# Pairs of PSUM banks as one tile in a block of causal attention and a gated feed-forward: one exp and one maximum per pair, the causal mask added by TensorE, and another place for the second half's maxima in the DMA queue

## The chip, the cores and the metric

The kernel runs on one core of one Trainium2 chip. The metric is device microseconds of that core, the median of several runs. Times inside the kernel come from one profiled execution, in microseconds (us) from the start of its span, or in ns where that is written.

## What is computed

Eight sequences (B) of 1024 tokens with 256 channels pass through a transformer block: a layer norm scaled and shifted per sequence, causal attention with 16 heads of 16 channels, a gated residual, a second modulated layer norm, and a feed-forward part that mixes each token with the one before it. The part that matters here:

```
scores = einsum("bhqd,bhkd->bhqk", q, k) * Hd ** -0.5
scores = where(causal, -inf, scores)
attn = softmax(scores)
out = einsum("bhqk,bhkd->bhqd", attn, v)
```

## The kernel before

**Tiling.** For each sequence `b` the heads are taken in four groups `s` of four. A group is worked off in twelve steps `t` (`COL_STEPS`). All engines walk the same list of (b, s, t), each with its own program in order, and semaphores tie them together. In the same steps stand the dense products of other parts of the block (projections for the next sequence, and output and feed-forward of the sequence before), so that a step holds attention work of three kinds and, mostly, a dense product.

**Column scores.** For a group's softmax weights TensorE makes scores with keys on partitions and queries along the free axis (`score_columns`, L1222 to L1240): `k_stack` is the stationary operand and `q_stack` the moving one, 64 rows each, so that an even head (rows 0 to 63) and an odd head (rows 64 to 127) use the two halves of the array at the same time. They go to two PSUM banks, `col_ps0` and `col_ps1`. A unit is one bank: one head where more than 256 queries are wanted, otherwise two. Eight of the twelve steps have four units, in two pairs; four steps have two units, one pair. ScalarE takes the exp of each unit (`exps`, L805 to L817), into `weights`. On diagonal blocks GpSimd sets the masked weights to zero (L664). TensorE multiplies the weights with `v_ones` (`values`, L1286), for step t in step t+1.

**Row maxima.** The softmax needs a maximum per query and head before the exp. It rides as two more rows of `q_stack`, and is worked out one group ahead: TensorE makes the scores of group s+1 with queries on partitions (`row_pair`, L1248 to L1269), into four banks `row_ps0` to `row_ps3`, and VectorE reduces them (`maximum`, L1021 to L1045). There are 40 units of one bank in a group, always an even and an odd one in a row. A unit whose block holds the diagonal goes through one masked add and maximum per head (L1035, a custom operation with `row_mask`, followed by a read of the accumulator); the others through a plain reduction (L1039). A group has 16 pairs of an even and an odd head whose block is diagonal. `split_max` (L1047 to L1067) then splits the maxima in two parts and turns them with one transpose of 128x32 in 32x32 blocks.

**The DMA queue.** SyncE issues nearly all transfers from one queue, in program order, and `hold` makes the whole queue wait. `fill_stacks` (L480 to L495) copies the next group's q and k into the stacks, twelve transfers per half of the tokens. `place_max` (L497 to L506) puts the turned maxima into `q_stack`, eight transfers per half: one for each 32 queries, for even and odd heads. Column scores of steps 0 and 4 wait for the two halves' maxima (L1226).

**TensorE's order in a step** (L1439 to L1465): the first pair of row scores (early), the first pair of column scores, the values of the step before, the second pair of row scores (late) if a dense product follows, the second pair of column scores, otherwise the late pair now, then the dense product.

## Time and profile before

| | |
|---|---|
| median of 3 runs | 1524.66 us (1518.13 to 1531.08) |
| profiled execution, its time | 1521.95 us |
| its span | 1520.0 us |
| busy PE, DVE, ACT, POOL | 1346.2, 1118.0, 958.2, 678.7 us |
| mean granted TensorE clock | 0.927 |

PE is TensorE, PEld its weight loads, DVE VectorE, ACT ScalarE, POOL GpSimd, SPq SyncE's DMA queue. Ends of matmuls are modelled and lie over each other, so that the time from one start to the next tells more than a duration. A granted clock of 1 is 2.4 GHz, of 0.5 it is 1.2 GHz.

### The profile page before, as it was taken

How to read it: one execution, taken by the hardware profiler on the slowest of the kernel's cores; microseconds unless marked ns; L12 is line 12 of the kernel's file. 1: busy time of each engine (PE TensorE's matmuls, PEld its weight loads, DVE VectorE, ACT ScalarE, POOL GpSimd, SP SyncE). 2: the span in 40 equal slices, each digit the busy share in tenths (PEclk: the TensorE clock that was granted, in tenths of full speed). 3: DMA queues.
4: the chain of work that ended last, by engine and by line, in shares of the span. 5: the costliest groups of instructions: out<-in, count | busy, mean ns of one | idle time of the engine just before them, and what ended most of it. 6: DMA issues, size and time to landing. Idle time of an engine off the chain costs nothing.

```text
span 1520.0 us, 28003 instructions
## 1 busy us (share of the span) xinstructions
PE 1346.2 (89%) x8744; PEld 746.3 (49%) x8744; DVE 1118.0 (74%) x3435; ACT 958.2 (63%) x1916; POOL 678.7 (45%) x1098
## 2 busy tenths in 40 slices
PE   5898889899998999889998899989998999998855
PEld 4443434455554555444554455545454555544444
DVE  8778667877678777877678777787778777777234
ACT  2167556766677666676677566776667666666633
POOL 4014122554436354553446545364546534343554
PEclk9598979999899999999899999999999898999878
DMA  4321124122331224222242223312232222221100
GB/s 139 75 64 47 42 50 112 49 65 68 84 86 46 54 66 118 67 54 55 67 108 53 56 70 97 82 44 54 72 105 63 64 54 76 68 58 50 38 29 28
DMA packets 90005, 101.77 MB, mean 67 GB/s; under 512 B 29681, under 2 KB 55545, under 8 KB 89857
## 3 DMA queue, kind: packets, MB, share of 16 engines
q1 hardware_dynamic: 89280, 99.20, 25.0%
q8 instruction: 70, 1.15, 0.3%
q10 hardware_dynamic: 576, 0.79, 0.3%
q14 instruction: 79, 0.64, 0.1%
HBM read 30.69 MB, written 8.94 MB: 26 GB/s over the span
## 4 chain that ended last, share of the span: by engine, by line
PE 51%; DVE 13%; SPq 10%; ACT 9%; issue 8%; POOL 7%; DMA 2%; ACTq 0%; POOLq 0%; DVEq 0%
PE val_ps L1286 13%; PE col_ps L1235 12%; PE row_ps L1264 9%; SPq L493 6%; ACT weights L815 5%; DVE row_ps L1035 5%; PE dense_ps L1296 4%; SPq L505 3%; PE dense_ps L1298 3%; PE dense_ps L1297 3%; PE dense_ps L1324 2%; DVE max_parts L1039 2%; POOL weights L664 2%; PE dense_ps L1339 2%; ACT xn_c L859 1%
## 5 line engine op out<-in xcount | busy, mean ns | idle before, releaser
L815 ACT ACTIVATE weights<-col_ps 128x512 f32<-128x512 f32 (+2 forms) x1280 | 643.7, 557 | 319.9 <-PE col_ps L1235 305.2
L1035 DVE CUSTOM_DVE_ANT_0 row_ps<-row_ps,row_mask 128x128 f32<-128x128 f32 (+3 forms) x1024 | 477.4, 517 | 209.7 <-PE row_ps L1264 209.3
L1235 PE MATMUL col_ps<-q_stack,k_stack 64*128 64x512 f32 (+3 forms) x1536 | 400.9, 410 | 36.1 <-ACT weights L815 20.4
L664 POOL TENSOR_SCALAR_AFFINE_SELECT weights<-weights 128x256 f32<-128x256 f32 x512 | 211.0, 425 | 460.1 <-ACT weights L815 458.7
L1039 DVE TENSOR_REDUCE max_parts<-row_ps 128x1 f32<-128x512 f32 x512 | 328.7, 681 | 86.5 <-PE row_ps L1264 84.8
L1286 PE MATMUL val_ps<-weights,v_ones 128*32 128x512 f32 (+3 forms) x3072 | 349.9, 529 | 25.6 <-POOL weights L664 18.1
L1264 PE MATMUL row_ps<-k_stack,q_stack 62*128 62x512 f32 (+3 forms) x1536 | 341.6, 434 | 29.3 <-DVE max_parts L1039 11.8
L1235 PEld LDWEIGHTS col_ps<-q_stack,k_stack 64*128 64x128 f32 x1536 | 210.5, 196 | 224.7 <-ACT weights L815 174.4
L1264 PEld LDWEIGHTS row_ps<-k_stack,q_stack 62*128 62x128 f32 x1536 | 163.8, 197 | 242.2 <-DVE max_parts L1035 79.9
L1035 DVE DVE_READ_ACCUMULATOR2_ANT max_parts<- 128x1 f32 x1024 | 144.7, 141 | 0.0
L1286 PEld LDWEIGHTS val_ps<-weights,v_ones 128*32 128x32 f32 x3072 | 62.1, 110 | 117.8 <-issue 61.6
L722 POOL TENSOR_TENSOR h_diff<-h 128x512 f32<-128x512 f32 x32 | 33.3, 1041 | 126.6 <-ACT h L878 125.9
L729 POOL TENSOR_TENSOR mix_lo<-mixed,mix_hi 128x512 fp32r<-128x512 f32 x64 | 81.7, 1298 | 17.5 <-ACT mix_hi L907 14.9
L1139 DVE SCALAR_TENSOR_TENSOR mixed<-h_diff,mus,h 128x256 f32<-128x256 f32 x128 | 63.8, 539 | 15.5 <-POOL h_diff L722 15.5
L1296 PE MATMUL dense_ps<-h_hi,w_hi 128*128 128x512 f32 x124 | 57.3, 462 | 3.0 <-POOL h_lo L639 1.6
L1298 PE MATMUL dense_ps<-h_hi,w_lo 128*128 128x512 f32 x124 | 51.7, 417 | 0.0
L733 POOL TENSOR_TENSOR k_lo<-k_sq,k_hi 128x512 fp32r<-128x512 f32 x28 | 39.3, 1404 | 26.4 <-ACT k_hi L912 25.9
L1297 PE MATMUL dense_ps<-h_lo,w_hi 128*128 128x512 f32 x124 | 51.0, 411 | 0.0
L888 ACT ACTIVATE h_diff<-dense_ps 128x512 f32<-128x512 f32 x28 | 16.7, 597 | 48.1 <-PE dense_ps L1345 48.1
L650 POOL TENSOR_SCALAR shift_c<-mv_c 128x2 f32<-128x2 f32 x32 | 8.5, 264 | 84.5 <-DVE mv_c L1076 84.1
L708 POOL TENSOR_TENSOR xq<-xq,gates_att 128x512 f32<-128x512 f32 x28 | 36.0, 1284 | 19.4 <-DMA xq<-in_x 19.3
L885 ACT ACTIVATE mix_out<-dense_ps 128x512 f32<-128x512 f32 x28 | 16.7, 598 | 38.4 <-PE dense_ps L1330 38.4
(194 smaller groups left out, 1893.8 us busy)
## 6 DMA issues: line engine op xcount, KB each, us to landing
q_stack<-q_part SPq DMA_DIRECT2D x384, 64.0 KB, 2.2
k_stack<-k_part SPq DMA_DIRECT2D x372, 64.0 KB, 2.2
xa<-in_x SPq DMA_DIRECT2D x8, 1024.0 KB, 5.6
q_stack<-max_rows SPq DMA_DIRECT2D x512, 2.0 KB
att<-val_out SPq DMA_DIRECT2D x64, 128.0 KB
recips<-recip_rows SPq DMA_DIRECT2D x32, 256.0 KB
xq<-in_x SPq DMA_DIRECT2D x28, 256.0 KB, 3.3
out<-xq SPq DMA_DIRECT2D x28, 256.0 KB, 2.1
```

The costliest lines, as they stand in the source:

```text
L493: sp.dma_start(stack[buf][at:at + HD, half].bitcast(F32), parts[part][lo:lo + 32, cols].bitcast(F32)).then_inc(stack_filled[buf][half], 16)
L664: nc.gpsimd.affine_select(out=w, in_=w, compare_op=ALU.is_ge, fill=0.0, base=0, pattern=[[0, 2], [1, P]], channel_multiplier=-1).then_inc( ...
L729: nc.gpsimd.tensor_tensor(mix_lo[:, m], mixed[:, m], mix_hi[:, m].bitcast(F32), ALU.subtract).then_inc(mix_lo_done, 1)
L815: nc.scalar.activation(weights[:, t % 2, heads[0]:heads[-1] + 1:2, 0:q1 - q0], col_ps[bank][:, 0:n * (q1 - q0)].rearrange("p (h q) -> p h ...
L1035: last = nc.vector.tensor_tensor_reduce(out=scores, in0=scores, in1=row_mask[:, HALF - width:HALF], scale=1.0, scalar=MASKED, op0=ALU.add, ...
L1039: last = nc.vector.reduce_max(dest, bank[:, 0:len(heads) * width].rearrange("p (h k) -> p h k", h=len(heads)), AX_X)
L1235: last = nc.tensor.matmul(col_ps[bank][:, i * (q1 - q0):(i + 1) * (q1 - q0)], stack_at(k_stack[s % 2], rows, heads[i], P * j, P * (j + 1)) ...
L1264: last = nc.tensor.matmul(banks[odd][:, n * width:(n + 1) * width], stack_at(q_stack[stack], rows, heads[n], P * i, P * (i + 1)), stack_at ...
L1286: last = nc.tensor.matmul(val_ps[32 * h:32 * h + 32, q0 - base:q1 - base], v_ones[:, j, G * s + h].rearrange("p d a -> p (d a)"), weights[ ...
L1296: nc.tensor.matmul(dst, a_hi(c), b_hi(c), start=(c == 0), stop=False)
L1297: nc.tensor.matmul(dst, a_hi(c), b_lo(c), start=False, stop=False)
L1298: last = nc.tensor.matmul(dst, a_lo(c), b_hi(c), start=False, stop=(c == KC - 1))
```

## The change

- The two column banks become one tile `col_ps` of two banks, and the four row banks two tiles of two banks. `exps` takes both units of a pair in one ACTIVATE of up to 1024 elements and waits for both; `maximum` reduces both units of a pair in one TENSOR_REDUCE and waits for both. The counts of semaphores stay, in steps of two.
- The custom masked maximum is gone. On diagonal blocks TensorE adds the mask to the scores in PSUM, with products of two bf16 constants (an identity and a triangle of -3e38), for even and odd heads side by side: per pair of heads four more matmuls, two with 128 columns and two with 64.
- The maxima are turned with four transposes of 32x32 into one tile of 32 partitions, so that `place_max` needs two transfers instead of eight.
- SyncE issues `place_max` of the second half right behind `fill_stacks`, ahead of the residual's load and the copies of values and sums.

The core of the diff:

```diff
-PLACED = 2 * (P // SQUARE) * 16
+PLACED = 2 * 16
 ...
+        col_pair = ps("col_ps", [P, COL_BANKS, HALF])
+        row_pair_ps = [ps(f"row_ps{i}", [P, 2, HALF]) for i in range(ROW_BANKS // 2)]
 ...
-                    for q in range(P // SQUARE):
-                        lo = SQUARE * q + 8 * MROWS * odd
-                        sp.dma_start(rows[:, :, q, :], max_rows[half][lo:lo + 8 * MROWS, :]
-                                     ).then_inc(max_placed[half], 16)
+                    sp.dma_start(stack[row:row + MROWS, half].rearrange("p g n -> p (g n)").bitcast(F32),
+                                 max_rows[half][8 * MROWS * odd:8 * MROWS * (odd + 1), :]).then_inc(max_placed[half], 16)
 ...
-                act.wait_ge(cols_ready, exp_index(b, s, c) + 1)
+                act.wait_ge(cols_ready, exp_index(b, s, c) + 2)
 ...
-                nc.scalar.activation(weights[:, t % 2, heads[0]:heads[-1] + 1:2, 0:q1 - q0],
-                                     col_ps[bank][:, 0:n * (q1 - q0)].rearrange("p (h q) -> p h q", h=n),
-                                     ACT.Exp, scale=SCALE).then_inc(exp_done, 1)
+                nc.scalar.activation(weights[:, t % 2, heads[0]:heads[0] + 2 * n, 0:q1 - q0].rearrange(
+                    "p (n o) q -> p o n q", o=2), col_pair[:, :, 0:n * (q1 - q0)].rearrange(
+                    "p o (n q) -> p o n q", n=n), ACT.Exp, scale=SCALE).then_inc(exp_done, 2)
 ...
-                        last = nc.vector.tensor_tensor_reduce(
-                            out=scores, in0=scores, in1=row_mask[:, HALF - width:HALF], scale=1.0, scalar=MASKED,
-                            op0=ALU.add, op1=ALU.max, accum_out=dest[:, n:n + 1])
+                nc.vector.reduce_max(dest, banks[:, :, 0:n * (k1 - k0)].rearrange("p o (n k) -> p o n k", n=n), AX_X
+                                     ).then_inc(max_done, 2)
 ...
-                nc.vector.transpose(max_rows[half][:], parts[:, 0:SQUARE].bitcast(F32)).then_inc(max_turned, 1)
+                for q in range(P // SQUARE):
+                    cols = slice(SQUARE * q, SQUARE * (q + 1))
+                    last = nc.vector.transpose(max_rows[half][:, cols], parts[cols, 0:SQUARE].bitcast(F32))
+                last.then_inc(max_turned, 1)
 ...
+                for n in range(len(pair[0])) if diagonal else ():
+                    for a in range(2):
+                        for odd in range(2):
+                            rows = slice(ROW_TILE * odd, ROW_TILE * (odd + 1))
+                            end = n == len(pair[0]) - 1 and a == 1
+                            last = nc.tensor.matmul(banks[odd][:, (n + 1) * width - P + ROW_TILE * a:(n + 1) * width],
+                                                    mask_ident[rows, a, :], mask_fill[rows, a, ROW_TILE * a:P],
+                                                    start=False, stop=end, skip_group_check=True)
+                            if end:
+                                last.then_inc(rows_ready, 1)
```

SyncE's part (`hold(max_turned, ...)` and `place_max(q_stack[s % 2], 1)` move up in `body`) is shown by its queue. Here is a group of the first sequence that also has back work; `xq` is the residual, `att` and `sums` the copies of values and sums. Before:

```order
L493 DMA k_stack0<-k_part0 16x2x512 x2
L493 DMA k_stack0<-k_part1 16x2x512 x2
L493 DMA k_stack0<-k_part0 16x2x512 x2
L534 DMA xq1<-in_x 128x2x256
L512 DMA att<-val_out1 64x512 [waits att_done,val_copied]
L514 DMA sums1<-val_out1 32x1x64
L505 DMA q_stack1<-max_rows1 2x8x32 [waits max_turned]
L505 DMA q_stack1<-max_rows1 2x8x32 x7
L539 DMA out<-xq0 128x2x256 [waits out_done]
```

The same place of the change:

```order
L496 DMA k_stack0<-k_part0 16x2x512 x2
L496 DMA k_stack0<-k_part1 16x2x512 x2
L496 DMA k_stack0<-k_part0 16x2x512 x2
L504 DMA q_stack1<-max_rows1 2x8x128 [waits max_turned]
L504 DMA q_stack1<-max_rows1 2x8x128
L533 DMA xq1<-in_x 128x2x256
L511 DMA att<-val_out1 64x512 [waits att_done,val_copied]
L513 DMA sums1<-val_out1 32x1x64
L538 DMA out<-xq0 128x2x256 [waits out_done]
```

The maxima move from behind three transfers and two waits to directly behind the fills, and are two rows instead of eight.

TensorE at steps 0 and 1 of a group (`row_ps` row scores, `col_ps` column scores, `val_ps` values). Before:

```order
L1235 MATMUL col_ps<-q_stack,k_stack 128x512 [waits exp_done,max_placed0]
L1235 MATMUL col_ps<-q_stack,k_stack 128x512 [waits exp_done]
L1286 MATMUL val_ps<-weights,v_ones 32x128 [waits sel_done]
L1286 MATMUL val_ps<-weights,v_ones 32x128 x3
L1235 MATMUL col_ps<-q_stack,k_stack 128x512 [waits exp_done] x2
L1264 MATMUL row_ps<-k_stack,q_stack 128x256 [waits max_done] x2
L1264 MATMUL row_ps<-k_stack,q_stack 128x256 x2
L1264 MATMUL row_ps<-k_stack,q_stack 128x384 [waits max_done] x2
L1235 MATMUL col_ps<-q_stack,k_stack 128x384 [waits exp_done] x2
```

The same place of the change:

```order
L1232 MATMUL col_ps<-q_stack,k_stack 128x512 [waits exp_done] x2
L1262 MATMUL row_ps<-k_stack,q_stack 128x256 [waits max_done] x2
L1262 MATMUL row_ps<-k_stack,q_stack 128x256 x2
L1273 MATMUL row_ps<-mask_fill,mask_ident 128x128 x2
L1273 MATMUL row_ps<-mask_fill,mask_ident 128x64 x2
L1273 MATMUL row_ps<-mask_fill,mask_ident 128x128 x2
L1273 MATMUL row_ps<-mask_fill,mask_ident 128x64 x2
L1262 MATMUL row_ps<-k_stack,q_stack 128x384 [waits max_done] x2
L1273 MATMUL row_ps<-mask_fill,mask_ident 128x128 x2
L1273 MATMUL row_ps<-mask_fill,mask_ident 128x64 x2
L1232 MATMUL col_ps<-q_stack,k_stack 128x384 [waits exp_done] x2
```

The order of scores and values is the same; behind each diagonal row pair there are four mask matmuls per pair of heads, ahead of the next column scores.

## Rows read from the trace of the kernel before

**Rows 1.** The page: busy us of each engine, share of the span, instructions
```profile
PE 1346.2 (89%) x8744; PEld 746.3 (49%) x8744; DVE 1118.0 (74%) x3435; ACT 958.2 (63%) x1916; POOL 678.7 (45%) x1098
```
**Rows 2.** The page's chain that ended last, by engine and by line
```profile
PE 51%; DVE 13%; SPq 10%; ACT 9%; issue 8%; POOL 7%; DMA 2%; ACTq 0%; POOLq 0%; DVEq 0%
PE val_ps L1286 13%; PE col_ps L1235 12%; PE row_ps L1264 9%; SPq L493 6%; ACT weights L815 5%; DVE row_ps L1035 5%; PE dense_ps L1296 4%; SPq L505 3%; PE dense_ps L1298 3%; PE dense_ps L1297 3%; PE dense_ps L1324 2%; DVE max_parts L1039 2%; POOL weights L664 2%; PE dense_ps L1339 2%; ACT xn_c L859 1%
```
**Rows 3.** Stretches: length, busy PE, PEld, DVE, ACT, POOL, then granted clock
```profile
40.00:70.00 30.00, 25.58 (x60) 13.77 (x60) 25.72 (x92) 2.31 (x5) 0.34 (x1) 0.50 0.35 63
500.00:700.00 200.00, 184.81 (x1239) 101.44 (x1238) 154.74 (x483) 135.41 (x273) 97.16 (x157) 0.96 0.26 68
```
**Rows 4.** Groups: line, engine, shapes, count, busy us, mean ns, idle before
```profile
L815 ACT ACTIVATE weights<-col_ps 128x512 f32<-128x512 f32 x896 | 488.1, 601 | 192.6 <-PE col_ps L1235 180.7
L1035 DVE CUSTOM_DVE_ANT_0 row_ps<-row_ps,row_mask 128x128 f32<-128x128 f32 (+3 forms) x1024 | 477.4, 517 | 209.7 <-PE row_ps L1264 209.3
L1035 DVE CUSTOM_DVE_ANT_0 row_ps<-row_ps,row_mask 128x512 f32<-128x512 f32 x256 | 172.1, 713 | 69.8 <-PE row_ps L1264 69.7
L1035 DVE CUSTOM_DVE_ANT_0 row_ps<-row_ps,row_mask 128x128 f32<-128x128 f32 x256 | 66.6, 320 | 24.8 <-PE row_ps L1264 24.8
L1039 DVE TENSOR_REDUCE max_parts<-row_ps 128x1 f32<-128x512 f32 x512 | 328.7, 681 | 86.5 <-PE row_ps L1264 84.8 <-issue 0.2
L1067 DVE STREAM_TRANSPOSE max_rows<-max_parts 128x32 f32<-128x32 f32 x64 | 13.5, 212 | 2.2
```
**Rows 5.** Timeline, a group's step 0: start, length, engine, line
```profile
670.85 0.30 PEld L1264 LDWEIGHTS row_ps<-k_stack,q_stack 62*128 62x128 f32 x4
...
671.07 0.19 PEld L1235 LDWEIGHTS col_ps<-q_stack,k_stack 64*128 64x128 f32 x2
...
671.61 2.27 ACT L815 ACTIVATE weights<-col_ps 128x512 f32<-128x512 f32 x4
...
672.26 0.18 PEld L1235 LDWEIGHTS col_ps<-q_stack,k_stack 64*128 64x128 f32 x1 [0.60 <-ACT weights L815]
...
672.75 0.18 PEld L1235 LDWEIGHTS col_ps<-q_stack,k_stack 64*128 64x128 f32 x1 [0.30 <-ACT weights L815]
```
**Rows 6.** Timeline, a step with a dense product of six matmuls
```profile
702.72 1.08 ACT L815 ACTIVATE weights<-col_ps 128x512 f32<-128x512 f32 x2
...
703.61 0.74 PE L1235 MATMUL col_ps<-q_stack,k_stack 64*128 64x512 f32 x2
...
704.15 1.09 ACT L815 ACTIVATE weights<-col_ps 128x512 f32<-128x512 f32 x2 [0.35 <-PE col_ps L1235]
704.28 0.19 PEld L1296 LDWEIGHTS dense_ps<-h_hi,w_hi 128*128 128x128 f32 x1 [0.24 <-issue]
```
**Rows 7.** Timeline, two matmuls of 512 columns behind each other
```profile
700.76 0.39 PE L1297 MATMUL dense_ps<-h_lo,w_hi 128*128 128x512 f32 x1
...
700.99 0.39 PE L1298 MATMUL dense_ps<-h_hi,w_lo 128*128 128x512 f32 x1
```
**Rows 8.** Timeline, SyncE's queue and TensorE up to step 4 of the group
```profile
676.95 0.50 SPq L534 DMA_DIRECT2D xq<-in_x  x1
...
678.91 5.27 SPq L505 DMA_DIRECT2D q_stack<-max_rows  x8
...
684.49 0.44 PE L1264 MATMUL row_ps<-k_stack,q_stack 62*128 62x128 f32 x3 [0.74 <-DVE max_parts L1039]
...
685.27 0.50 PE L1235 MATMUL col_ps<-q_stack,k_stack 64*128 64x512 f32 x2 [0.35 <-DMA q_stack<-max_rows]
```
**Rows 9.** Waits: who waited for whom, us in total, times, longest
```profile
PE col_ps L1235 <- DMA q_stack<-max_rows: 12.8, 10, 3.1
```
**Rows 10.** The chain in order of time, start of a group s = 1
```profile
627.89 0.32 DVE row_ps L1035
...
629.04 1.01 DVE att_n L1154
...
632.20 0.62 DVE stats_a L1072 x2
```

More of the change, by code:

```diff
@@ L160, in build @@
         max_parts = [sb(f"max_parts{i}", [P, P], F32R) for i in range(2)]
-        max_rows = [sb(f"max_rows{i}", [P, 2 * MROWS * 8]) for i in range(2)]
+        max_rows = [sb(f"max_rows{i}", [SQUARE, P]) for i in range(2)]
         val_out = [sb(f"val_out{i}", [P, HALF]) for i in range(2)]
@@ L919, in body @@
                     units = range(COL_FIRST[t], COL_FIRST[t + 1]) if attends(kind) else ()
-                    for c in units[:2]:
+                    for c in units[:1]:
                         exps(b, s, t, c)
@@ L924, in body @@
                     normalise_next(b, kind, s, t)
-                    for c in units[2:]:
+                    for c in units[2::2]:
                         exps(b, s, t, c)
@@ L1180, in body @@
                         empty_dense(*item)
-                    for u in early[1:]:
-                        maximum(b, s, u)
                     for item in at:
                         mix(*item)
-                    for u in late:
+                    for u in late[::2]:
                         maximum(b, s, u)
@@ L1262, in row_pair @@
                         rows = slice(ROW_TILE * odd, ROW_TILE * odd + MAX_AT)
-                        end = n == len(heads) - 1
+                        end = n == len(heads) - 1 and not diagonal
                         last = nc.tensor.matmul(banks[odd][:, n * width:(n + 1) * width],
@@ L1269, in row_pair @@
                             last.then_inc(rows_ready, 1)
+                for n in range(len(pair[0])) if diagonal else ():
+                    for a in range(2):
+                        for odd in range(2):
+                            rows = slice(ROW_TILE * odd, ROW_TILE * (odd + 1))
+                            end = n == len(pair[0]) - 1 and a == 1
[4 more added lines that the diff above has]
+                                last.then_inc(rows_ready, 1)
             def values(b, s, t):
```

61 lines of the change are left out of this document (29 added, 32 removed).

## The prediction

> **What bounds the kernel now.** The page's first part comes first: TensorE is busy 89% of the span, VectorE 74%, ScalarE 63% [rows 1]. The chain that ended last says that this is not TensorE alone: half of it (51%) is TensorE, 13% VectorE, 10% SyncE's queue, 9% ScalarE, 7% GpSimd [rows 2]. So I read stretches. In the middle (500 to 700 us) TensorE is busy 185 of 200 us at a granted clock of 0.96, close to the 2.4 GHz level; in the opening (40 to 70 us) VectorE and TensorE are both busy for 25.6 and 25.7 of 30 us, but at a clock of 0.50, the 1.2 GHz level, and there only row scores and maxima run [rows 3]. The reader is to see that in the middle work added to TensorE is paid unless it falls into one of its waits, and that work taken from VectorE or ScalarE pays only where TensorE waits for it.
>
> The timeline of a step shows two such patterns. In a step with a dense product [rows 6] the second pair of column scores starts at 703.61 and its second matmul stands waiting for the second exp (0.74 us for the pair against 0.50 for a pair that starts together [rows 8]); the dense product follows at 704.28 and hides the exps from 704.15 on. In a step without one [rows 5] the four exps run as one unbroken chain of 2.27 us, because TensorE gets the first bank back 0.49 us ahead of the second (672.26 and 672.75) and refills it while ScalarE works on the other.
>
> **The change part by part. The mask on TensorE.** 16 pairs of heads per group, 32 groups, are 512 pairs of heads, each with two pairs of matmuls (128 and 64 columns). No row shows a bf16 operand. From above: row pairs of 128 columns go at the pace of their loads, two pairs from 670.85 until the next load at 671.07, so 0.11 us a pair and 0.22 per pair of heads [rows 5]. From below: 512 columns take 0.23 us from start to start [rows 7], so 128 take 0.057 and 64 take 0.028, together 0.085, if the loads are hidden. The first mask load can hide behind the row product, but the load of whatever follows cannot hide behind 64 columns; and the operand has half the bytes. No row says whether a load goes by bytes or by columns, so I take the middle, 0.15.
>
> The Trainium skill bears on this (TensorE: Matmul & The Clock Gate, section on weight-path perf modes): it says that loads of 128 columns in a type other than fp32 are made about twice as fast. By that, the load of a mask would take an estimated 0.055 us and a pair of heads about 0.165 (0.055 and then the next fp32 load's 0.11); by the row it is 0.22. No row here shows which; by the first the term below would be 58 us, by the second 77.
>
> On the path lie those in steps where TensorE is not waiting anyway. In twelve steps they stand as 4, 2, 2, 0, 2, 0, 2, 1, 1, 0, 1, 1. The two late ones of step 0 run behind the second column scores while the exps are awaited, and I count three more as absorbed by waits (step 4, and in groups s = 1 and 3 where chains of other engines end last). That leaves 11 of 16: 32 x 11 x 0.15 = **53 us more**.
>
> **One exp per pair.** Two exps of 512 behind each other take 1.08 us [rows 6], one takes 0.60 [rows 4]; another 512 elements add 0.48 to that from the same two rows, or a little less without the second start, so one of 1024 is worth about 1.04, a gain of 0.04 a pair. The price is that TensorE gets both banks at once. From the start of a load to the first exp are 0.54 us (671.07 to 671.61 [rows 5]), and this gap can no longer lie beside an exp: two pairs take 1.04 + 0.55 + 1.04 = 2.63 us instead of 2.27, **0.36 us more**, wherever nothing else lies in between. With a dense product it costs nothing: the second pair's second matmul waited for the second exp already, TensorE reaches the dense product at the same 704.28, and the exps end 0.1 us later beside 1.4 us of dense work [rows 6, 7]. If that cover were gone it would cost the same 0.36. By the program, 10 of the 48 steps of a sequence have four units and no dense product. Eight sequences: 80 x 0.36 = **29 us more**. What is queued behind the waiting column scores on TensorE are the late rows and the next step; who waits for them are ScalarE and VectorE.
>
> **One maximum per pair.** The busy time of maxima is 477.4 + 328.7 = 806 us [rows 4]. The reads of the accumulator lie within. One column more costs (172.1 - 66.6) / 256 / 384 = 1.07 ns, a reduction of 512 costs 328.7 / 512 = 0.64 us, so one of 1024 costs 1.19 and one of 768 costs 0.92. A group has 14 pairs of 1024, 4 of 768 and 2 of 512: 21.6 us, 691 in all, 115 less. Three more transposes per half, at most 0.21 each [rows 4], give back up to 40. So VectorE is relieved of some 75 us, but it waits for row scores for 210 + 87 us already [rows 4], so this counts only where it ends last. One place is the opening, where it is as busy as TensorE [rows 3]: about 4 us. The other is the start of group s = 1, where from 627.89 to 632.20 eight masked maxima and one other operation of 1.01 are the chain [rows 10]: 3.3 us become 0.64 + 1.19, 1.4 less, in seven sequences 10 us. **14 us less.** A first pair of maxima now stands whole ahead of the dense unit's emptying on VectorE, where only half of it did: that emptying comes 0.5 us later. TensorE claims the dense bank again only behind two pairs of column scores and the values, and the masks delay it by as much; I take nothing.
>
> **The placement of maxima.** Eight transfers take 5.27 us of the queue, 0.66 each, and stand behind 1.96 us of residual, values and sums (676.95 to 678.91) [rows 8]. Two take 1.3, so the second half's maxima land 5.9 us earlier, and the last wait of column scores at step 4 goes: 12.8 us in ten waits [rows 9]. Next in line there is VectorE, which held the row scores ahead of it 0.74 us [rows 8], and that stays. Values and sums come 1.3 us later by the move, with a whole group until the next use of their buffer, so nothing. **13 us less.** The exps that are on the chain (5% of the span [rows 2], 76 us or some 66 pairs) give 3 us by their 0.04, and fewer long waits of TensorE may leave it at 2.4 GHz a little more often; 5 us for that is a guess from the 4% missing in the clock [rows 3]. Together **8 us less**. GpSimd gets a few small operations more, once, at its start, where the loads of weights and tokens are under way; I take nothing.
>
> **Sum.** 53 + 29 - 14 - 13 - 8 = +47 on the profiled execution's 1521.95 us (1520.0 span and 1.95 around it), which is 2.7 below the median of the runs: 1569, and with half of that difference **1570 us**.
>
> **Rivals.** *The reliefs win* (other side). If the mask products cost only their columns (0.085) and half of them fall into waits, they are 256 x 0.085 = 22 us; the coupling in half of its steps 15; and if half of the 115 us that the maxima lose lies on the path, 57, with 13 and 8 as above, the sum is -41: 1481 us. It decides where more than about 95 us of relief reach the path against the full 53 and 29. For it speaks that VectorE is 13% of the chain and SyncE's queue 10% [rows 2]; against it that VectorE waits for TensorE far more than the other way round [rows 4]. *Nothing that can be measured*: masks at 0.10 (35 us) and coupling 29 against 60 of relief, +4: 1526. *Lockstep everywhere*: if the dense products do not hide the coupling, it is paid in all eight four-unit steps of each group, 256 x 0.36 = 92, and the masks fully, 512 x 0.22 = 113; with 35 of relief +170: 1692. Against it speaks the second matmul that waits already [rows 6].
>
> **How the numbers follow.** I give the forecast 0.55, nothing measurable 0.20, the reliefs 0.15, lockstep 0.10. A measurement of this kernel tells about 1% from no change, which is 1509 to 1540. So faster 0.15, same 0.20, slower 0.65. The forecast's own range, with masks between 0.085 (30 us) and 0.22 on all (113), is 1540 to 1630. The range to be given reaches from 1510 to 1630: below it lies most of the reliefs' 0.15, above it most of lockstep's 0.10, about 0.2 together.
>
> **What would show it.** In the profile after: the mask line's matmuls with about 0.15 us per pair of heads from the end of the row product's columns to the next start; in a step 0 a gap near 0.55 us on ScalarE between its two exps; no wait of column scores for the placements of maxima; VectorE's busy share down to about 68%, with more waiting for row scores; the first row maxima earlier in the opening. The prediction is wrong if the mask loads are hidden (then TensorE's time hardly grows), if ScalarE's gaps show up behind dense products too, or if stretches where other engines end last shorten by more than 1.5 us per group.

## The result, and the profile after

The changed kernel takes 1573.8 us (median of 4 runs, 1570.8 to 1579.7) against 1522.8 us for the kernel before (1518.1 to 1531.1): a ratio of 1.0333 with a 95% interval of 1.0278 to 1.0389. A second comparison later gave 1.0279 (1.0244 to 1.0314). So the change costs 43 to 51 us; forecast were 47. The profiled execution has 1573.96 us, a span of 1572.1. Two executions on record ran in a slower state of the chip, one of the kernel before (1546.32 us) and one of the kernel without masks at the old place (1508.59 us), and the ratios leave them out.

Two lines of the page: busy us by engine, and the chain that ended last by engine:

```profile
PE 1311.9 (83%) x10792; PEld 740.3 (47%) x10792; DVE 1057.9 (67%) x1707; ACT 919.4 (58%) x1276; POOL 673.9 (43%) x1102
...
PE 50%; ACT 18%; DVE 14%; issue 10%; POOL 6%; DMA 1%; SPq 1%; ACTq 1%; POOLq 0%; DVEq 0%
```

Every engine is busy for less time than before [rows 1], TensorE too, although it has 2048 matmuls more, and yet the span is 52 us longer: what grew is waiting. (TensorE's sum is of modelled durations, at a mean granted clock of 0.938 for 0.927, so it does not say what the masks cost.) On the chain ScalarE went from 9 to 18% and SyncE's queue from 10 to 1% [rows 2]. The groups by line, busy us and mean ns, then the idle time before them with what ended it, say where:

```profile
L1036 DVE TENSOR_REDUCE max_parts<-row_ps 128x2 f32<-128x1024 f32 (+3 forms) x640 | 704.7, 1113 | 399.1 <-PE row_ps L1273 307.1 <-PE row_ps L1262 90.6 <-issue 0.2
L819 ACT ACTIVATE weights<-col_ps 128x1024 f32<-128x1024 f32 (+2 forms) x640 | 600.3, 938 | 425.9 <-PE col_ps L1232 383.4 <-issue 39.1
L1232 PE MATMUL col_ps<-q_stack,k_stack 64*128 64x512 f32 (+3 forms) x1536 | 306.3, 423 | 114.9 <-ACT weights L819 112.4
L1232 PEld LDWEIGHTS col_ps<-q_stack,k_stack 64*128 64x128 f32 x1536 | 143.4, 194 | 267.3 <-ACT weights L819 259.7 <-issue 1.0
L1273 PE MATMUL row_ps<-mask_fill,mask_ident 64*128 64x128 bf16 (+1 forms) x2048 | 115.4, 214 | 0.0
L1273 PEld LDWEIGHTS row_ps<-mask_fill,mask_ident 64*128 64x128 bf16 x2048 | 58.0, 99 | 40.8 <-issue 24.9
L1065 DVE STREAM_TRANSPOSE max_rows<-max_parts 32x32 f32<-32x32 f32 x256 | 51.2, 200 | 4.9
```

The exps (L819) and the column scores (L1232) wait for each other: ScalarE 383 us for scores, and the scores' matmuls 112 us for exps. Before, the matmuls waited 20 us for exps and 13 us for placements [rows 9]:

```profile
ACT weights L815 <- PE col_ps L1235: 305.2, 254, 25.2
...
PE col_ps L1235 <- ACT weights L815: 20.4, 59, 0.7
```

The wait for placements is gone. The maxima take 705 us instead of 806 [rows 4], close to what was worked out (691), and the four transposes 51 instead of 13.5.

### The profile page after: what moved, and what is told of

It is laid out like the page before. It is cut to its first block, busy times and chain, and to the rows that moved or that the text cites. A ratio compares the mean times of both kernels' runs of the same rounds, so it can differ in the third digit from the quotient of the medians.

```text
span 1572.1 us, 30252 instructions
## 1 busy us (share of the span) xinstructions
PE 1311.9 (83%) x10792; PEld 740.3 (47%) x10792; DVE 1057.9 (67%) x1707; ACT 919.4 (58%) x1276; POOL 673.9 (43%) x1102
## 4 chain that ended last, share of the span: by engine, by line
PE 50%; ACT 18%; DVE 14%; issue 10%; POOL 6%; DMA 1%; SPq 1%; ACTq 1%; POOLq 0%; DVEq 0%
ACT weights L819 13%; PE col_ps L1232 12%; PE val_ps L1294 9%; PE row_ps L1262 8%; DVE max_parts L1036 8%; PE dense_ps L1304 4%; PE dense_ps L1332 3%; PE dense_ps L1305 3%; PE dense_ps L1306 3%; POOL weights L669 2%; PE row_ps L1273 2%; PE dense_ps L1347 2%; PE dense_ps L1323 2%; ACT xn_c L863 2%; POOL mix_lo L734 1%
## 5 line engine op out<-in xcount | busy, mean ns | idle before, releaser
L1036 DVE TENSOR_REDUCE max_parts<-row_ps 128x2 f32<-128x1024 f32 (+3 forms) x640 | 704.7, 1113 | 399.1 <-PE row_ps L1273 307.1
L819 ACT ACTIVATE weights<-col_ps 128x1024 f32<-128x1024 f32 (+2 forms) x640 | 600.3, 938 | 425.9 <-PE col_ps L1232 383.4
L1232 PE MATMUL col_ps<-q_stack,k_stack 64*128 64x512 f32 (+3 forms) x1536 | 306.3, 423 | 114.9 <-ACT weights L819 112.4
L1262 PE MATMUL row_ps<-k_stack,q_stack 62*128 62x512 f32 (+3 forms) x1536 | 302.0, 426 | 26.0 <-DVE max_parts L1036 17.8
L1232 PEld LDWEIGHTS col_ps<-q_stack,k_stack 64*128 64x128 f32 x1536 | 143.4, 194 | 267.3 <-ACT weights L819 259.7
L1262 PEld LDWEIGHTS row_ps<-k_stack,q_stack 62*128 62x128 f32 x1536 | 143.5, 194 | 218.4 <-issue 127.5
L1273 PE MATMUL row_ps<-mask_fill,mask_ident 64*128 64x128 bf16 (+1 forms) x2048 | 115.4, 214 | 0.0
L1138 DVE SCALAR_TENSOR_TENSOR mixed<-h_diff,mus,h 128x256 f32<-128x256 f32 x128 | 65.0, 548 | 20.4 <-POOL h_diff L727 20.4
L1273 PEld LDWEIGHTS row_ps<-mask_fill,mask_ident 64*128 64x128 bf16 x2048 | 58.0, 99 | 40.8 <-issue 24.9
L1065 DVE STREAM_TRANSPOSE max_rows<-max_parts 32x32 f32<-32x32 f32 x256 | 51.2, 200 | 4.9
L713 POOL TENSOR_TENSOR xq<-xq,gates_att 128x512 f32<-128x512 f32 x28 | 35.9, 1284 | 25.8 <-DMA xq<-in_x 25.8
L1304 PE MATMUL dense_ps<-w_hi,h_hi 128*128 128x256 f32 x120 | 38.2, 318 | 5.8 <-DVE xq L1121 5.8
```

Of the source, the lines that this page charges most:

```text
L819: nc.scalar.activation(weights[:, t % 2, heads[0]:heads[0] + 2 * n, 0:q1 - q0].rearrange("p (n o) q -> p o n q", o=2), col_pair[:, :, 0:n ...
L1036: nc.vector.reduce_max(dest, banks[:, :, 0:n * (k1 - k0)].rearrange("p o (n k) -> p o n k", n=n), AX_X).then_inc(max_done, 2)
L1138: last = nc.vector.scalar_tensor_tensor(mixed[:, m, c, :], h2_diff[:, c, :], mus[:, m, c:c + 1], h2[s % 2][:, c, 0:QT], ALU.mult, ALU.add)
L1232: last = nc.tensor.matmul(col_ps[bank][:, i * (q1 - q0):(i + 1) * (q1 - q0)], stack_at(k_stack[s % 2], rows, heads[i], P * j, P * (j + 1)) ...
L1262: last = nc.tensor.matmul(banks[odd][:, n * width:(n + 1) * width], stack_at(q_stack[stack], rows, heads[n], P * i, P * (i + 1)), stack_at ...
L1273: last = nc.tensor.matmul(banks[odd][:, (n + 1) * width - P + ROW_TILE * a:(n + 1) * width], mask_ident[rows, a, :], mask_fill[rows, a, RO ...
```

## The experiments

All ratios are to the kernel before, run beside each kernel; 1% is 15.3 us of its median of some 1529 us. Differences between two kernels are differences of such ratios. A stretch in the tables below runs from the first product of one step's values to that of the next; "behind step 5" is the stretch that starts with the values of step 5. It holds the second pair of column scores and the dense product of step 6.

### An exp for each bank again

In the changed kernel (PE, SyncE and VectorE as they are):

```diff
-                act.wait_ge(cols_ready, exp_index(b, s, c) + 2)
+                act.wait_ge(cols_ready, exp_index(b, s, c) + 1)
...
-                nc.scalar.activation(weights[..., heads[0]:heads[0] + 2 * n, ...], col_pair[:, :, ...], ...).then_inc(exp_done, 2)
+                nc.scalar.activation(weights[..., heads[0]:heads[-1] + 1:2, ...], col_ps[bank][...], ...).then_inc(exp_done, 1)
...
-                    for c in units[:1]:
+                    for c in units[:2]:
```

> The changed kernel with one thing undone: each column bank has its own exp again (640 become 1280), the first bank is freed half an exp earlier. Masks on TensorE, paired maxima, two transfers per placement and their early place stay. Theory A, the terms of the prediction: the coupling costs 29 us less the 3 us of exps that were on the chain, so 26 come back: about 1548 us. Theory B, which the trace after suggests (ScalarE's waits for column scores grew from 305 to 383 us, TensorE's waits for exps to 112): the coupling is the larger term, 50 to 60 us, and the masks the smaller: about 1515 to 1522. Rival C, coupling free: stays at 1574. In A and B the wait of column scores for exps falls from 112 us to near the 20 of before.

Measured: 1517.05 us, ratio 0.9924 (0.9895 to 0.9954). The pairing of exps is worth the whole loss and more: 3.6 to 4.1%, some 54 to 63 us. That is theory B for the coupling. The waits, us in total, times, longest:

```profile
ACT weights L820 <- PE col_ps L1233: 305.7, 360, 25.7
...
PE col_ps L1233 <- ACT weights L820: 19.8, 61, 0.7
```

Both are back where they were before (305.2 and 20.4).

The price shows in a step without a dense product. Timeline of step 0 of a group in the changed kernel, start and length in us, the idle time before in brackets:

```profile
832.56 1.02 ACT L819 ACTIVATE weights<-col_ps 128x1024 f32<-128x1024 f32 x1 [0.35 <-PE col_ps L1232]
...
833.64 0.19 PEld L1232 LDWEIGHTS col_ps<-q_stack,k_stack 64*128 64x128 f32 x2 [1.11 <-ACT weights L819]
833.64 0.50 PE L1232 MATMUL col_ps<-q_stack,k_stack 64*128 64x512 f32 x2 [0.84 <-ACT weights L819]
...
834.22 0.35 PE L1273 MATMUL row_ps<-mask_fill,mask_ident 64*128 64x128 bf16 x8
834.26 1.02 ACT L819 ACTIVATE weights<-col_ps 128x1024 f32<-128x1024 f32 x1 [0.68 <-PE col_ps L1232]
```

The exp ends at 833.58, TensorE starts to load 0.06 later, and the second exp starts at 834.26: a gap of 0.68 us, of which 0.62 lie between the load and the exp. That is longer than the 0.54 of [rows 5]. This exp needs both banks, but the two matmuls start together, so the wait for the second explains little of the 0.08, and what does stays open. The two exps span 832.56 to 835.28, 2.72 us, where four took 2.27 [rows 5].

### The mask products left out

In the changed kernel:

```diff
-                diagonal = k1 == P * (i + 1)
+                diagonal = False
```

> The changed kernel without the mask products on TensorE: the row maxima are then taken over the whole diagonal tile, so this kernel leaves the mask out. Paired exps and all else stay. Theory A, the prediction's term: 0.15 us per pair of heads on 11 of 16, 53 us come back: about 1521. Theory B: the loads of the masks are nearly hidden, 0.085 per pair of heads, 30 us or less come back: 1544 or more. Rival C: each product and the next load cost their full loads, 0.22: about 1496.

Measured: 1562.1 us, ratio 1.0209 (1.0168 to 1.0250); the changed kernel in its two comparisons 1.0333 and 1.0279. The masks cost 11 to 19 us in the changed kernel, the smaller with intervals that overlap. That is on theory B's side, and below the 30 us that it had as its most. Two stretches of one sequence show where they cost and where not (length, busy PE, PEld, DVE, ACT, POOL, granted clock, DMA share, GB/s). The changed kernel, from the values of step 10 to those of step 11, and from those to the next group's:

```profile
829.31:832.38 3.07, 3.07 (x35) 2.28 (x35) 2.46 (x9) 1.20 (x2) 0.77 (x2) 1.00 0.28 64
832.38:835.92 3.54, 2.15 (x32) 1.30 (x31) 1.80 (x2) 2.68 (x4) 0.81 (x2) 1.00 0.45 103
```

The same two without masks:

```profile
815.39:818.23 2.84, 2.84 (x26) 2.05 (x27) 2.32 (x9) 0.98 (x2) 0.77 (x2) 1.00 0.30 69
818.23:821.78 3.55, 1.78 (x21) 0.97 (x19) 2.00 (x3) 2.74 (x5) 0.82 (x2) 1.00 0.43 100
```

In the first TensorE never waits, and two pairs of heads cost 0.23 us, 0.115 each. In the second three pairs of heads cost nothing (3.54 and 3.55): their columns lie in the gap that the paired exp opens. The granted clock over the whole span fell as well, from 0.938 to 0.909 in the profiled executions (in the others 0.926 to 0.942 with masks, 0.907 to 0.921 without). So some stretches are longer without the masks, at the lower clock. Behind step 3 of group 1, with masks and then without:

```profile
666.00:669.55 3.55, 1.90 (x18) 0.86 (x17) 3.41 (x8) 2.72 (x4) 3.24 (x6) 1.00 0.22 74
650.39:654.55 4.16, 2.79 (x18) 1.27 (x16) 3.58 (x9) 2.90 (x5) 3.60 (x6) 0.67 0.19 63
```

Part of what the masks cost is given back that way; how much was not measured.

### The old place in SyncE's queue

In the changed kernel, hold and place_max of the second half go back behind residual, values and sums:

```diff
-                    if attends(kind):
-                        hold(max_turned, b * (2 * G) + (2 * s + 2))
-                        place_max(q_stack[s % 2], 1)
                     if backs(kind) and kind != "drain":
                         load_residual(b, s)
...
+                    if attends(kind):
+                        hold(max_turned, b * (2 * G) + (2 * s + 2))
+                        place_max(q_stack[s % 2], 1)
                     if attends(kind) and s == G - 1:
                         load_gates(b)
```

> The changed kernel with SyncE's issue of the second half's maxima put back behind residual, values and sums. Two transfers per placement stay. Theory A: two transfers instead of eight end about 4.0 us earlier by themselves (0.66 us each), more than the mean stall of 1.28 us that the column scores had, so the place in the queue is worth nothing: 1574, within 3 us. Rival B: the place is what took the stall away: 12.8 us come back, about 1587, and a wait of column scores for the placements stands in the profile again in about ten steps.

Measured: 1567.18 us, ratio 1.0253 (1.0215 to 1.0291), not above the changed kernel (1574, to be met within 3, was 7 us off). No wait of column scores for placements shows up. Two transfers at the old place are early enough, so rival B falls; no gain of the new place shows, and it may cost some us.

### The changed kernel beside the others

> The changed kernel once more, beside the others, to compare it with the one that has the old place (1.0253). Theory A: the early place costs a little, since residual and values stand behind it: 1.033 again. Rival B: the difference was that of two jobs: 1.025 to 1.028.

Measured: 1570.83 us, ratio 1.0279 (1.0244 to 1.0314). That is in rival B's range. Against 1.0253 at the old place it is within the intervals: the place is worth between nothing and a loss of 0.8%; the sign stays open.

### The new place alone, in the kernel before

The same lines moved up in the kernel before, where place_max issues eight transfers.

> The kernel before with one thing of the change alone: SyncE issues the second half's eight transfers of maxima behind the stack fills, ahead of residual, values and sums. Theory A: they land about 1.96 us earlier, more than the mean stall of 1.28 us in ten steps, so 10 to 13 us are gained: about 1511. Rival B: residual, values and sums now come 5.3 us later, and what they feed (residual into the dense step, values into the next buffer) waits: no gain or a loss, 1523 or more. Rival C: the stall was hidden behind another wait, 1523.

Measured: 1650.08 us, ratio 1.0792 (1.0753 to 1.0830): 121 us slower. Rival B had the mechanism, but nobody had the size. The waits in it:

```profile
PEld val_ps L1286 <- POOL weights L664: 165.2, 127, 6.0
POOL xq L708 <- DMA xq<-in_x: 146.1, 28, 7.7
PE val_ps L1286 <- POOL weights L664: 131.7, 51, 5.9
```

and the same in the kernel before:

```profile
PEld val_ps L1286 <- POOL weights L664: 48.6, 110, 1.5
...
POOL xq L708 <- DMA xq<-in_x: 19.3, 17, 2.4
PE val_ps L1286 <- POOL weights L664: 18.1, 38, 1.4
```

The residual xq is issued behind eight transfers and so comes late. GpSimd waits for it in 28 steps, and behind that wait in GpSimd's queue stand the selects of the diagonal weights; TensorE's values wait for these, 114 us more. The granted clock of the span fell to 0.875. It is the transfers that make the residual late, some 5.3 us of the queue each time, and not the wait for the turned maxima that now stands ahead of it too: SyncE waited for those twice, once for 18.3 us.

```profile
SPq L131 <- DVE max_rows L1067: 27.5, 2, 18.3
```

With two transfers ahead of it the same order is nearly free: GpSimd's wait for the residual is 25.8 us in the changed kernel, and 1.8 with the old place.

### An exp for each bank at the old place

Both edits above together in the changed kernel.

> The changed kernel with two things undone: an exp per column bank, and the second half's maxima issued behind residual, values and sums again. What stays of the change: masks on TensorE, paired maxima, four transposes and two transfers per placement. Theory A, the effects add: 0.76% below the kernel before from the exps alone, and 6 us more from the old place: about 17 us below the kernel before, ratio 0.989. Rival B: the old place helped only because TensorE stood in the coupling; then the ratio stays at 0.992 or rises.

Measured: 1516.9 us, ratio 0.9922 (0.9895 to 0.9948), the same as with the new place. Theory A's 0.989 lies just outside the interval; with an exp per bank no worth of the place can be measured. Taking the pairing of exps from the kernel at the old place gives 1.0253 - 0.9922 = 3.3%, 51 us.

### The same without masks

> As the kernel with an exp per bank and the old place, but without the mask products: the maxima are taken over whole diagonal tiles, so the mask is left out. It prices the masks where the coupling doesn't hide them. Theory A: in the steps of the trace a pair of heads cost 0.09 to 0.135 us, so 352 on the path give back 32 to 48 us: ratio to the kernel before about 0.965. Rival B: as with paired exps, a TensorE with less to do is granted a lower clock (0.909 against 0.938 there) and gives most of it back: ratio within 0.012 of the kernel with the masks.

Measured: 1498.89 us, ratio 0.9793 (0.9738 to 0.9848). Here the masks cost 1.3%, 20 us, short of theory A and at the edge of what B allowed (1.2%). The granted clock is 0.952 against 0.966 with them in the profiled executions; over all executions in the ratios the medians are 0.951 and 0.960, and their ranges overlap. So the masks look dearer where exps don't open gaps for them, and cost some two fifths of the term forecast.

This is the quickest kernel of all those measured. One thing follows for the mask: GpSimd still sets the masked weights to zero behind the exp, and in exact arithmetic a softmax does not depend on which maximum is subtracted, so a maximum over the whole tile will do as long as masked scores aren't so much larger that the exps of the others vanish. For which inputs that holds no run here shows.

### Two transfers and four transposes alone, in the kernel before

```diff
-PLACED = 2 * (P // SQUARE) * 16
+PLACED = 2 * 16
...
-                nc.vector.transpose(max_rows[half][:], parts[:, 0:SQUARE].bitcast(F32)).then_inc(max_turned, 1)
+                for q in range(P // SQUARE):
+                    cols = slice(SQUARE * q, SQUARE * (q + 1))
+                    last = nc.vector.transpose(max_rows[half][:, cols], parts[cols, 0:SQUARE].bitcast(F32))
+                last.then_inc(max_turned, 1)
```

with place_max as in the changed kernel, at its old place.

> The kernel before with one thing of the change: four transposes per half instead of one, and two transfers per placement instead of eight, at their old place in SyncE's queue. Theory A: the stall of 12.8 us in ten waits goes, since the transfers end about 4 us earlier, and what stands behind the 5.3 us of eight transfers (loads of tokens, the next stack fills) comes earlier too: 10 to 15 us less, ratio 0.991. Rival B: the three more transposes (40 us of VectorE in all) stand in front of the next maxima and eat the gain: ratio 0.997 or more.

Measured: 1537.87 us, ratio 1.0067 (1.0040 to 1.0094): 10 us slower. The wait for placements is gone and nothing is gained. TensorE's matmuls of row scores wait longer for maxima instead:

```profile
PE row_ps L1263 <- DVE max_parts L1035: 24.3, 33, 1.3
...
PE row_ps L1263 <- DVE max_parts L1031: 9.1, 13, 2.3
```

In the kernel before:

```profile
PE row_ps L1264 <- DVE max_parts L1039: 11.8, 17, 0.9
...
PE row_ps L1264 <- DVE max_parts L1035: 5.8, 10, 1.0
```

That is 33.4 us for 17.6. The transposes stand in VectorE's order ahead of maxima whose banks TensorE needs. Behind step 2 of group 3 of one sequence (length, busy PE, PEld, DVE, ACT, POOL, granted clock, DMA share, GB/s), in the kernel before and then with the four transposes:

```profile
904.25:907.23 2.98, 2.11 (x18) 1.00 (x17) 2.95 (x7) 0.66 (x2) 2.26 (x4) 1.00 0.07 23
915.27:918.85 3.58, 2.04 (x18) 0.93 (x16) 3.47 (x10) 0.66 (x2) 2.85 (x4) 1.00 0.29 73
```

VectorE is busy nearly all the time in both, and the stretch is 0.60 us longer, as much as three more transposes of 0.2 us. Behind step 2 of groups 0, 2 and 3 it is longer in most sequences. The lower clock behind them comes and goes between executions, so the 10 us were not added up from them.

### One exp per pair alone, in the kernel before

> The kernel before with one thing of the change: one exp over both column banks. Prices the coupling alone. Theory A, as it came out of the changed kernel: about 0.55 us in each four-unit step without a dense product and some more around it, 50 to 57 us: ratio about 1.035. Theory B, the prediction's working: 0.36 us in 80 steps, less 3: ratio 1.017. Rival C: the coupling costs only beside the masks, ratio 1.005 or less.

Measured: 1565.55 us, ratio 1.0249 (1.0210 to 1.0287): 38 us, between theories A and B. TensorE's column scores wait 116.2 us for exps. Rival C falls: the masks are not needed for the coupling.

### One transpose and eight transfers, with paired maxima

The kernel with an exp per bank at the old place, with the transposes and transfers of the kernel before.

> The changed kernel with three things undone: an exp per bank, the old place in SyncE's queue, and one transpose with eight transfers per placement. What stays of the change: masks on TensorE and one maximum per pair of banks. Theory A, effects add: two transfers with four transposes cost 0.67% in the kernel before, so without them 0.9922 - 0.0067 = 0.9855 of the kernel before. Rival B: paired maxima have taken VectorE off that path, so the transposes cost nothing now, and the ratio stays at 0.992. Rival C: with eight transfers the wait of the column scores for placements comes back and costs 13 us: 1.000.

Measured: 1526.41 us, ratio 0.9992 (0.9966 to 1.0018), 0.7% above the kernel with two transfers: rival C. The wait is back:

```profile
PEld col_ps L1234 <- DMA q_stack<-max_rows: 10.2, 8, 3.2
PE col_ps L1234 <- DMA q_stack<-max_rows: 8.9, 8, 3.0
```

So the same edit costs 10 us in the kernel before and gains 11 with paired maxima and masks on TensorE. The reading is that VectorE was next in line there and no longer is here; which of the two took it out of line was not tested apart.

### One maximum per bank

The kernel with an exp per bank at the old place, with maxima of one bank each; masks on TensorE, transposes and transfers stay as in the change. With it the second maximum of a step's first pair stands behind the emptying of the dense bank again, as in the kernel before.

```diff
-                dve.wait_ge(rows_ready, at + 2)
+                dve.wait_ge(rows_ready, at + 1)
...
-                nc.vector.reduce_max(dest, banks[:, :, 0:n * (k1 - k0)]..., AX_X).then_inc(max_done, 2)
+                nc.vector.reduce_max(dest, bank[:, 0:len(heads) * (k1 - k0)]..., AX_X).then_inc(max_done, 1)
```

> The kernel with an exp per bank and the old place (ratio 0.992), with the pairing of maxima undone as well: one maximum per bank, 1280 instead of 640; masks on TensorE, four transposes and two transfers stay. It prices the pairing. Theory A, what the sum of the other runs leaves: masks 20, transposes 10, and 42 us of gain by the paired maxima, so 1.02 of the kernel before. Theory B, the prediction: 14 us, ratio 1.001. In A the stretches behind step 2 of groups 2 and 3, where the granted clock fell in the kernel before, are long again.

Measured: 1545.41 us, ratio 1.0100 (1.0068 to 1.0132). The pairing of maxima gains 1.8%, 27 us: between the theories, and twice what the prediction gave to all of the maxima. Stretches around step 2 of group 2 show it (columns as above). Maxima of one bank each:

```profile
868.89:872.51 3.62, 2.27 (x27) 1.15 (x25) 3.55 (x9) 0.67 (x3) 2.89 (x4) 1.00 0.00 0
872.51:877.39 4.88, 4.88 (x23) 2.91 (x22) 3.25 (x10) 3.20 (x6) 1.29 (x4) 0.65 0.22 78
```

Paired maxima:

```profile
855.41:857.61 2.20, 1.94 (x26) 0.97 (x25) 2.17 (x4) 0.66 (x2) 1.55 (x3) 1.00 0.00 0
857.61:861.54 3.93, 3.37 (x25) 1.95 (x23) 3.69 (x8) 3.22 (x6) 1.75 (x2) 1.00 0.20 66
```

And the kernel before:

```profile
859.06:862.85 3.79, 2.28 (x16) 1.03 (x16) 3.79 (x13) 0.26 (x1) 3.26 (x4) 0.88 0.02 3
862.85:868.82 5.97, 5.97 (x24) 3.30 (x23) 2.72 (x9) 3.26 (x6) 1.47 (x5) 0.51 0.21 70
```

In the kernel before VectorE is busy all 3.79 us of the first stretch and TensorE only 2.28. Then the granted clock falls to 0.51, the 1.2 GHz level, and the next stretch takes 5.97 us instead of 3.93. That this is the clock shows in the kernel before itself, where the second sequence has the same stretch at 1.00:

```profile
334.06:337.99 3.93, 3.93 (x24) 2.05 (x23) 3.47 (x16) 3.22 (x6) 1.45 (x2) 1.00 0.20 67
```

The long step is paid twice: by the wait, and by the clock behind it. It is not so in every sequence: behind step 3 of group 2 the kernel before has 5.16 to 5.97 us at 0.51 to 0.70 in six of eight, and with paired maxima two of eight are that long. The Trainium skill (TensorE: Matmul & The Clock Gate, section on HAM oscillation) tells of the same for waits on transfers: work behind a long wait starts at the lower clock. The trace agrees, 0.51 behind a wait that is on another engine, VectorE.

### One exp per pair only beside a dense product

The kernel with an exp per bank at the old place, paired where a four-unit step has a dense product:

```diff
+                dense_at = {(unit[0], unit[1]) for unit in dense_units(b, kind)}
...
+                    both = len(units) == 4 and (s, t) in dense_at
+                    for c in units[:2:2 if both else 1]:
+                        exps(b, s, t, c, both)
```

> The kernel with an exp per bank and the old place (ratio 0.992), but with one exp per pair of banks in the four-unit steps that have a dense product behind the second column scores, and only there. Theory A, the prediction's step: beside a dense product the pairing costs nothing, and it saves ScalarE a start: 0.992, or up to 3 us less. Rival B: part of the 51 us of pairing was paid in those steps too: 1.00 or more. In A the four-unit steps with a dense product last as long as with an exp per bank (3.61 and 3.87 us behind steps 5 and 7 of group 0), and those without one 3.0 instead of 3.55.

Measured: 1523.65 us, ratio 0.9964 (0.9942 to 0.9986) against 0.9922 without any pairing: between the theories, nearer to A. Stretches behind steps 5 and 7 of group 0 and step 5 of group 3, with this pairing, and (the third) behind step 11 of group 0, which has no dense product and an exp for each bank here:

```profile
783.69:787.27 3.58, 3.01 (x23) 1.32 (x21) 2.92 (x4) 3.39 (x6) 0.00 (x0) 1.00 0.50 165
791.48:795.37 3.89, 3.69 (x22) 1.69 (x20) 2.46 (x4) 2.54 (x3) 0.82 (x2) 1.00 0.41 95
804.76:807.77 3.01, 2.54 (x32) 1.60 (x31) 1.31 (x2) 2.80 (x6) 0.81 (x2) 1.00 0.46 106
...
913.12:916.67 3.55, 2.99 (x21) 1.32 (x20) 1.77 (x3) 3.39 (x6) 3.34 (x5) 1.00 0.01 2
```

The same with an exp for each bank:

```profile
776.67:780.29 3.62, 3.05 (x23) 1.48 (x21) 2.98 (x4) 3.52 (x8) 0.00 (x0) 1.00 0.58 169
784.55:788.42 3.87, 3.87 (x23) 1.87 (x21) 2.45 (x4) 2.67 (x5) 0.83 (x2) 1.00 0.44 102
797.80:800.80 3.00, 2.53 (x32) 1.59 (x31) 1.30 (x2) 2.80 (x6) 0.82 (x2) 1.00 0.46 107
...
906.99:910.31 3.32, 3.22 (x21) 1.35 (x20) 2.03 (x3) 3.25 (x8) 3.17 (x5) 1.00 0.01 2
```

Steps 5 and 7 last the same with one exp or two (3.58 and 3.62, 3.89 and 3.87), and the step without a dense product is at 3.0 again. In a few others, as behind step 5 of group 3, the pairing costs 0.2 to 0.3 us although work on the dense bank is there. The difference in all is 0.4%, 6 us, with intervals that just overlap; it was not followed further. So most of the 51 us that the pairing of exps costs come from the other steps: the four-unit steps without such work, and the steps of two units, which have an exp for each bank in this kernel as well.

## Why the prediction was right

The time, 1574 for a forecast 1570, is right; the sum under it is right only as a whole, since errors of its terms cancel. That they cancel to within a few us is luck. What was rightly seen is that the change loses, that the coupling of the exps and the masks cost more than the reliefs give, and where the coupling is paid. One way of adding up the change, from the kernel before to the changed one, each step from two measured ratios:

| step | ratio after it | us | the prediction's terms |
|---|---|---|---|
| four transposes, two transfers | 1.0067 | +10 | -13, with the place |
| masks from VectorE to TensorE, one maximum per bank | 1.0100 | +5 | +53, less a part of 14 |
| one maximum per pair | 0.9922 | -27 | part of -14 |
| one exp per pair | 1.0253 | +51 | +29, less 3 |
| the new place | 1.0279 | +4, not clear of noise | in the -13 |

The second row is a difference of two edits at once (1.0100 - 1.0067) and within both intervals; the others stand on one edit each. Another order gives other numbers, because the effects don't add: transfers and transposes cost 10 us in one kernel and gain 11 in another, and the pairing of exps costs 38 and 51, there with intervals that overlap.

**The masks, 53 forecast.** The direction was right; of the size some two fifths or less are left. A pair of heads costs 0.115 us where TensorE is the bound, not 0.15, and nothing in the steps where an exp is awaited. Taken out, they give back 20 us with an exp per bank and 11 to 19 in the changed kernel. The rule of the Trainium skill cited ahead of the result (TensorE: Matmul & The Clock Gate, weight-path perf modes) agrees on the load, 99 ns recorded for a bf16 load against 194 for fp32; but the estimate from it, 0.165 a pair, is too high. The 0.115 lies nearer to the 0.085 that the prediction gave to the columns alone, so most of the loads seems to lie beside columns.

**The coupling, 29 forecast.** It is the largest term, not the second. The mechanism was as described: a gap between two exps in steps without a dense product, next to nothing in most steps with one. Three things were mis-sized. First, the gap is 0.68 us, not 0.55: 0.62 from the load to the exp where the working took 0.54, and TensorE's start behind the first exp, 0.06, which it left out. Second, the end of the chain moves the next step's first column scores as well, since they need both banks: such a step lasts 3.54 us for 3.00, 0.54 more and not 0.36. That holds for step 0 of a group, and for most of the same kind at step 4. At steps 8 and 9 most are 0.03 to 0.31 longer. Behind step 8 of group 0, which holds step 9, with an exp for each bank and then in the changed kernel (columns as above):

```profile
788.42:791.39 2.97, 2.90 (x24) 1.28 (x22) 2.94 (x5) 2.47 (x7) 0.82 (x2) 1.00 0.46 105
822.90:825.96 3.06, 2.56 (x25) 1.04 (x23) 3.03 (x5) 2.35 (x5) 0.81 (x2) 1.00 0.46 107
```

Third, there are more such steps than 80. The 10 are right for the middle sequences, but by the program the first has 18, the second 11 and the last 19, since part of the dense work of their neighbours is missing there: 98 in all. Added up stretch by stretch, from the profiled execution with an exp for each bank (new place) to that of the changed kernel's second comparison, the 98 are 40 us longer, 0.41 each, of the 50 by which the spans differ; in the kernel before, with and without the pairing, 38 of 45. So the term should have been about 40. The rest lies in the other steps, mainly four-unit steps beside dense products, which the prediction had free; what makes it was not found.

**The maxima, 14 less forecast.** The busy time was right (705 us for 691), and the place of the gain was not: it was sought in the opening and at the start of group s = 1. The opening gained nothing: in the trace TensorE's first values start at 75.5 us of the span, before at 73.8, and the first maximum at 45.0 for 44.0. Without the masks the first values start at 72.3, so there, at a granted clock of 0.50, the masks take more than the maxima give. The gain lies mainly around step 2 of groups 2 and 3, where VectorE was full and TensorE fell to the lower clock behind it. "It waits for row scores already, so this counts only where it ends last" was the right rule; the prediction looked for such places in two stretches alone, and named the price of the clock as a guess of 5 us.

**The placement, 13 less forecast.** This step failed. The wait was indeed gone, as forecast, but VectorE stood next in line, which the prediction said too, and yet it counted the full 12.8 us as gain. In the kernel before the edit costs 10 us, as TensorE waits longer for maxima behind three more transposes; the prediction had put them off the path as a part of 75 us of relief. Only with paired maxima and masks on TensorE do two transfers gain about what was forecast, 11 us. The earlier place in the queue, which was to bring 1.96 of the 5.9 us by which the maxima land earlier, gives nothing that shows.

**The last 8 less.** Neither part was found. The 3 us by longer exps don't show: with exps paired beside dense products alone the time is 6 us longer, barely clear of noise, and not shorter. The 5 us by the clock were a guess; the granted clock is 0.938 for 0.927, and no run tells what that alone is worth.

**SyncE's queue.** "Values and sums come 1.3 us later, so nothing" was right as far as the waits show, in which nothing for these two grew by more than 0.2 us, but the residual was left out of that sentence. With two transfers it is late by little (GpSimd waits 25.8 us for it, 19.3 before, 1.8 with two transfers at the old place); with eight, as the kernel before with the new place shows, the loss is 121 us.

**The rivals.** The reliefs did win by more than thought: without the pairing of exps the other parts together are 12 us faster than before, so the other side had the right sign for the change without that one edit, though not its size (12 us, not 41). Lockstep everywhere is refuted by steps 5 and 7, which pairing left as long as they were, though a few steps with a dense product did pay 0.2 to 0.3 us.

**The signs.** The gap of exps (0.68), the placements without a wait and VectorE's share (67%) came as named or near it, and VectorE waits 398 us for row scores instead of 294. The masks cost 0.115 a pair instead of 0.15, and the first maxima are not earlier. One sign of being wrong showed in part: TensorE's busy time did not grow, and the masks' loads are in good part hidden.

## What to carry to other kernels

Joining two instructions across both buffers of a pair saves a start and takes away the double buffering: count the gap from the consumer's last element to the producer's first, at each place where nothing else stands between, and at the next step's start too. Relief of an engine was worth here what its longest burst cost the bound engine, and that was the wait and the lower clock behind it; read it step by step, not by busy shares. Count the steps of the first and the last round apart from the middle ones, where work of a neighbour is missing. A transfer that is moved ahead in an in-order queue delays everything behind it, and an engine that waits for one of those delays all that stands behind in its own queue: keep the number of transfers small before moving them up. The quickest version with the mask is the change without the pairing of exps, 0.8% below the kernel before (0.9895 to 0.9954).

## What the runs showed of the hardware

A pair of heads' mask, four bf16 matmuls of 128 and 64 columns accumulated onto an fp32 product, cost 0.115 us of TensorE's time in a stretch where it never waited, less than two of the four recorded loads (99 ns each) one behind the other. And TensorE with less to do had the lower granted clock: 0.909 without masks against 0.938 with them, in all executions of the two kernels alike; with an exp per bank it was 0.951 against 0.960 in the median, with ranges that overlap.
